# Moving ACT's copy of a head's product from behind the first to behind the second exponential of the next head

## The reference

```python
x = _layernorm(x + _L0_attn_ref(x, ...))           # causal, 2048 keys, rotary
x = _layernorm(x + _L0_xattn_ref(x, ctx, mask))    # 1601 keys, masked
x = _layernorm(x + _L0_ffn_ref(x, ...))            # fp8 linear
x = _layernorm(x + _L1_attn_ref(x, ...))           # causal, 2048 keys, with an MLP
x = _layernorm(x + _L1_xattn_ref(x, ctx))          # 1601 keys, no mask
x = _layernorm(x + _L1_ffn_ref(x, ...))            # top-2 of 8 experts and a shared one
```

```python
scores = scale * jnp.einsum('bhqd,bhkd->bhqk', q, k)     # masked where the layer has a mask
attn = jax.nn.softmax(scores, axis=-1)
out = jnp.einsum('bhqk,bhkd->bhqd', attn, v)             # then the heads side by side @ Wo + bo
```

## Time and profile before

| | |
|---|---|
| time, median of 3 (lowest to highest) | 2999.99 us (2996.73 to 3009.27) |
| the profiled execution's own time | 3006.59 us |
| its span, first to last instruction | 3004.8 us |
| PE matmuls busy | 2786.9 us, 93% of the span |
| DVE busy | 2157.4 us, 72% |
| ACT busy | 1822.5 us, 61% |
| POOL busy | 544.2 us, 18% |
| mean granted TensorE clock | 0.952 of full speed |
| line 480, exponentials | 1600, 1535.7 us busy |
| line 453, copies of a head's product | 64, of 597 ns (median) |

### The profile page before, as it was taken

One profiled execution on the slowest core, in us unless ns is written; L12 is line 12 of the kernel. 1 busy time (PEld: TensorE's weight loads), 2 busy tenths in 40 slices (PEclk: granted clock), 3 DMA queues, 4 the chain that ended last, 5 costly groups with the idle time before them and its releaser, 6 DMA issues. The chain is left out here.

```text
span 3004.8 us, 93752 instructions
## 1 busy us (share of the span) xinstructions
PE 2786.9 (93%) x39186; PEld 1029.0 (34%) x39187; DVE 2157.4 (72%) x5870; ACT 1822.5 (61%) x2158; POOL 544.2 (18%) x760
## 2 busy tenths in 40 slices
PE   4999999999999999976999999999999999899998
PEld 2622222522222222233322223563222222256664
DVE  7689887488888788746798895227999999652114
ACT  2288878536667666753488887323878877931222
POOL 0188880120000000001222212303000000002330
PEclk7899999979999999997999999997999999989999
DMA  3344441311100111011211111102122221112112
GB/s 98 115 123 133 129 121 42 110 29 26 26 20 20 26 27 26 20 27 41 75 42 41 43 42 49 53 20 66 25 53 69 62 56 33 36 59 65 43 44 87
DMA packets 120407, 166.79 MB, mean 56 GB/s; under 512 B 38228, under 2 KB 89311, under 8 KB 119985
## 3 DMA queue, kind: packets, MB, share of 16 engines
q1 hardware_dynamic: 102192, 117.21, 14.4%
q0 software_dynamic: 12320, 43.02, 4.8%
q10 hardware_dynamic: 5472, 0.56, 0.2%
HBM read 126.51 MB, written 26.72 MB: 51 GB/s over the span
## 5 line engine op out<-in xcount | busy, mean ns | idle before, releaser
L747 DVE TENSOR_REDUCE mpart<-ps 128x1 f32<-128x512 f32 x1536 | 980.3, 683 | 115.2 <-PE ps L555 111.3
L555 PE MATMUL ps<-stack 48*32 48x512 f16 (+6 forms) x13312 | 952.1, 354 | 35.7 <-DVE mpart L747 12.2
L480 ACT ACTIVATE xT<-ps,exp_scale 128x1024 f32<-128x1024 f32 (+3 forms) x800 | 793.7, 1029 | 261.8 <-PE ps L594 121.5
L480 ACT ACTIVATE cn<-ps,exp_scale 128x1024 f32<-128x1024 f32 (+4 forms) x800 | 742.0, 960 | 212.8 <-PE ps L576 99.1
L576 PE MATMUL ps<-stack 50*32 50x512 f16 (+3 forms) x11648 | 756.2, 377 | 64.1 <-ACT xT L480 46.6
L555 PEld LDWEIGHTS ps<-stack 48*32 48x32 f16 x13312 | 282.4, 91 | 1015.5 <-DVE mpart L747 506.0
L740 DVE CUSTOM_DVE_ANT_0 scrap<-ps,arena 128x401 bf16<-128x401 f32 (+1 forms) x1024 | 534.3, 574 | 128.1 <-PE ps L555 128.1
L616 PE MATMUL ps<-xT,vall 128*17 128x512 f32 (+4 forms) x3648 | 421.3, 523 | 2.2 <-POOL xT L439 1.4
L616 PE MATMUL ps<-cn,vall 128*17 128x512 f32 (+3 forms) x3392 | 412.1, 507 | 1.0 <-ACT cn L480 1.0
L576 PEld LDWEIGHTS ps<-stack 50*32 50x32 f16 x11648 | 189.0, 90 | 215.1 <-ACT xT L480 115.7
L734 DVE CUSTOM_DVE_ANT_0 scrap<-ps,scrap 128x128 bf16<-128x128 f32 (+3 forms) x512 | 247.3, 484 | 16.7 <-PE ps L555 12.5
(11 more groups left out here) (282 smaller groups left out, 2548.8 us busy)
## 6 DMA issues: line engine op xcount, KB each, us to landing
stack<-q_parts SPq DMA_DIRECT2D x384, 64.0 KB, 2.7
stack<-k_parts SPq DMA_DIRECT2D x192, 64.0 KB, 2.8
wbuf<-in_maskT POOLq DMA_DIRECT2D x24, 512.0 KB, 4.4
arena<-in_moe_w SPq DMA_DIRECT2D x19, 512.0 KB, 4.6
stack<-k_parts SPq DMA_DIRECT2D x192, 50.0 KB, 2.3
stack<-sums_inverse SPq DMA_DIRECT2D x16, 512.0 KB, 5.6
parts<-osb SPq DMA_DIRECT2D x240, 32.0 KB
wbuf<-in_mask POOLq DMA_DIRECT2D x16, 401.0 KB, 3.8
```

Of the source, the lines that this page charges most:

```text
L480: nc.scalar.activation(e.prob[tile % P_SLOTS][0:rows, half * HALF + first:(half + 1) * HALF], S_PS(g)[0:rows, first:HALF], ACT.Exp, scale= ...
L555: last = nc.tensor.matmul(bank[quarter(j), i * w:i * w + w], qs[b][rows, at:at + 32], ks[b][rows, a:a + w], start=True, stop=True)
L747: nc.vector.tensor_reduce(dst, src, AX, ALU.max).then_inc(unit_used, 1)
```

## The change

The copy is issued behind the exponential of slot 1 of the next head, where it was issued behind that of slot 0. Nothing else differs: the same instructions with the same waits, and the copy and one exponential change places on ACT, 15 times in each stage.

```diff
                         nc.scalar.activation(e.prob[tile % P_SLOTS][0:rows, half * HALF + first:(half + 1) * HALF],
                                              S_PS(g)[0:rows, first:HALF], ACT.Exp,
                                              scale=e.exp_scale[0:rows, layer:layer + 1]).then_inc(exp_done, 1)
-                        if n == 0 and h:
+                        if n == 1 and h:
                             copy_out(h - 1)
                 copy_out(H - 1)
```

## The result

The kernel after takes 2952.65 us (median of 4, 2951.35 to 2953.88), the one before 3000.05 us (median of 4, 2996.73 to 3009.27): a ratio of 0.9837, 95% interval 0.9815 to 0.9859. The forecast was 2950, and 52.5 us less than the profiled execution before; the spans of the two profiled executions, 3004.8 and 2950.7 us, are 54.1 apart.

A forecast was written before the change was run, and what follows sets the result against it. PE was taken to pace the stages, stalling at changes of heads. Stalls of 32.9 us plus 19.6 of the clock made 52.5, off 3006.59 (2954.1) or the median 2999.99 (2947.5); 2950 was taken, range 2938 to 2972.

The forecast's parts named there:

- The reading of the stall: At each change of heads ACT holds a ready exponential behind the waiting copy; PE's slot 3 scores stall, 46.6 us in all.
- Stage 4: Cross attention without mask: 0.82 us saved at each of 14 changes of heads, 0.6 at the last; 12.1 us.
- Stage 2: Masked cross attention, PE full: 0.47 us of PE's issue saved at each of 15 changes; 7.0 us, bounds 3.6 to 8.7.
- Stage 1: Causal attention: 0.47 us saved at each of 15 changes, limited by DVE's hole; 7.0 us, bounds 0 and 9.9.
- Stage 3: Causal attention: 0.45 us saved at each of 15 changes if ACT hands it on; 6.8 us, bounds 0 and 7.4.
- The clock: PE's clock falls go with the stall: 16.2 us in stage 4, 3.4 in stages 1 and 3; 19.6 together.
- The falls stayed: Rival: PE's clock falls have another cause and remain, only the stalls go; 2967 us, chance 0.17.
- The stall only moves in the causal stages: Rival: stages 1 and 3 give nothing from stalls, ACT having almost no idle time before the copy; 2965 us, chance 0.12.
- Nothing won: Rival: DVE takes over at once as the bound, so the time stays at 3000 us; chance 0.07.
- Slower, as the product waits for the copy: Rival: a head's first product on PE waits for the later copy, up to 24 us lost; 3015 or so, chance 0.04.

The follow-up runs named there:

- stall_mid: Kernel after plus an ACT copy of 1664 scratch columns onto itself behind the exponential of slot 12 in stage 4's heads: 2967.55 us.

## Why the prediction was right, and where it was off

**The reading of the stall was right.** An exponential that was ready stood behind a copy that wasn't; putting it in front took PE's gap away in stages 2 and 4 and left 0.36 of 1.01 us in stage 1 and 0.38 of 0.86 in stage 3. SP's later transfers cost nothing that shows.

**Stage 4.** 12.1 us of stalls and 16.2 of the clock were forecast. The change of heads went from 3.32 to 2.50 us, and the last one from 3.11 to 2.24: 14 x 0.82 + 0.87 = 12.4. The stage is 28.3 us shorter in all, from 540.3 to 512.0, from its first product to its last. I had put the next bound at the 2.50 of an ordinary pair, and it is met to a hundredth.

**Stage 2.** 7.0 forecast, 7.7 measured (662.5 to 654.8). The reading of unit to mask, 0.47 instead of the gap of 0.24, is what made it right; the gap alone would have said half. The rest is the last change, into the head without units, which gained 0.92.

**Stage 1.** 0.47 forecast at each change, bounded by DVE's hole; 0.44 measured, 2.64 to 2.20. The hole is closed, as said.

**Stage 3 is the term that was mis-sized:** "15 x 0.45 = 6.8 us". The change of heads went from 2.63 to 2.35 us, 0.28 each, 4.2 us. I asked whether ACT can hand the shift on, and by ACT it could: its gap of 0.34 before slot 4 has all but gone. I didn't ask who holds the unit before the first product. PE and DVE after, against the earlier trace rows:

```profile
1507.71 0.41 PE L576 MATMUL ps<-stack 50*32 50x512 f16 x8 [0.38 <-ACT xT L480]
1507.95 0.58 PE L555 MATMUL ps<-stack 48*32 48x256 f16 x8
1508.46 1.05 PE L616 MATMUL ps<-xT,vall 128*17 128x512 f32 x8
```

```profile
1507.38 1.29 DVE L747 TENSOR_REDUCE mpart<-ps 128x1 f32<-128x512 f32 x2 [1.49 <-PE ps L555]
```

The scores are now 0.48 us sooner, but the product follows them by 0.75 us where it took 0.55 (1548.65 to 1549.20). DVE starts on the first maximum at 1507.38 and is done with it 0.69 us later, at 1508.07; there are three banks, so the unit before the product waits for that one. Moving one unit ahead of the scores starts DVE sooner, at 0.98 us of idle time for 1.49, and the product follows the scores by 0.58 again: the missing 0.17 is found. That the second unit moved as well adds nothing fits with the exponential of slot 1 as the bound from there.

**The clock: the size right, the cause half told.** The forecast said that the falls come of the stall and go with it: 19.6 us. They went, all of them, in all four stages of the profiled execution. The four stages are 53.1 us shorter together (10.7, 7.7, 6.4 and 28.3), and the changes of heads make 6.6 + 7.6 + 4.2 + 12.4 = 30.8 of it, so by subtraction some 22 us are the clock's, 15.9 of them in stage 4. In stages 1 and 3 I had counted half of the falls as lost and half as kept, for the half stall that is left (and had overlooked one in the last head of stage 1). All were lost here; but of the eight traces of kernels with the copy at slot 1 in these stages and PE's order as it was, four have one fall left, in the last head of stage 1 or 3.

But "each fall comes right behind a change of heads" was read as "behind the stall", and `stall_mid` shows that this is too little: 14 stalls of 0.93 us in mid-head brought none. In stage 4 it takes the smaller matmuls of the 65-key tile beside it. In stages 1 and 3, where the last tiles of a head are narrow instead, that is argued and not tested. The sign of the change was safe either way, since the change takes away one of the two things that have to meet.

On what the Trainium skill says (page "TensorE: Matmul & The Clock Gate"): the section "HAM oscillation — how this bites in real kernels", which ties falls to waits on transfers, would have kept them, and the measurement decides against it here. Its next section, "A second HAM failure mode: psum-queue depth-cycling", on short idles between groups of matmuls, fits; that the size of the matmuls around them counts is shown by the runs and not by that section.

**How near the total came is in part luck.** The stalls gave 30.8 us for 32.9, the clock 22 for 19.6, and the two misses cancel. The sum fits the execution that it was read from (54.1 us won for 52.5), which had more falls than its like; by the medians 47.4 are won.

**The rivals.** The falls stayed: no, in no stage. The stall only moves in the causal stages: no, 0.44 and 0.28 of it were won, though the 0.28 is that rival in part. Nothing won: no. Slower, as the product waits for the copy: not at slot 1; one slot further on it is so, with a stall of 0.82 us in front of line 616 where 0.7 to 0.8 was expected.

## What to carry to other kernels

Where an engine takes its work in order, don't put an instruction that waits for the youngest result in front of one whose input is ready; but find the first reader of what is delayed, and count the room to it, here between one exponential and two. To size such a change, compare an interval across the place with the same interval in the ordinary case, on the engine that is full, rather than taking the gap that the profile prints; and ask of every piece between the stall and the next landmark who frees its buffer. A short stall in a place where the matmuls are small anyway can cost more by the clock than by itself: in stage 4 here 15.9 us against 12.4.

## What the runs showed of the hardware that was not expected

The clock of TensorE fell from 2.4 to 1.2 GHz at stalls of 0.93 us where matmuls of 65 rows and fewer column groups stood just before them (6 falls at 14 such stalls, in each of two kernels), and not once at 28 such stalls with full tiles around them. With full tiles it fell only at the one longer stall of each stage, 1.76 us. At 0.50 us beside the thin tile it fell 4 times in stage 4; at 0.65 us beside the thin tile of stage 2, not at all. Each fall lasted 3.4 or 6.8 us of the clock's record, and in the kernel before a head that had one was 1.1 to 2.6 us longer. The falls in the causal stages of kernels with the same code there numbered 4 to 7 from one execution to the next, those in stage 4 6 to 9, worth 4 to 5 us there. That fits with the narrower spread of the kernel after, 2.5 us for 12.5 in the first runs; on another chip it was 5.9 for 8.3.
